# A transformer block on one core: another order of work on TensorE, VectorE, ScalarE and GpSimd in its attention part

## What is computed

```
x = L0_attn_x                                   # (8, 512, 256)
h = _layernorm(x) * (1 + ca) + sa
x = x + ga * _L0_attn_ref(h, w_qkv, w_out)      # q, k = elu(rope(q * SCALE)) + 1, elu(rope(k * SCALE)) + 1
   # for each row: kv += k v^T; ks += k; out = q kv / max(q ks, 1e-6)
h = _layernorm(x) * (1 + cb) + sb
x = x + gb * _L0_ffn_ref(h, router_w, w1, w2)   # top 2 of 8 experts
```

## Time and profile before

| | before |
|---|---|
| median of three runs | 779.57 us |
| lowest and highest | 779.16 and 779.76 us |
| span of the profiled execution | 776.0 us |
| PE, DVE, ACT, POOL busy over the span | 92%, 81%, 74%, 67% |
| attention part (start to the last chunk's offset, by the trace) | about 336 us |
| 24 steps of it, from `f` of chunk 2 to `f` of chunk 26 | 228.6 us |

### The profile page before, as it was taken

How to read it: one execution, slowest core, us unless ns; L and a number is a source line. 1 busy time by engine, 2 the same in 40 slices (tenths; PEclk the granted TensorE clock), 3 DMA queues, 4 the chain that set the end, 5 groups by cost and what they waited for, 6 DMA issues and landing times.

```text
span 776.0 us, 24871 instructions
## 1 busy us (share of the span) xinstructions
...
## 2 busy tenths in 40 slices
...
GB/s 226 113 67 133 110 135 120 131 120 139 124 140 116 151 64 67 120 48 8 96 77 69 71 73 74 76 70 79 70 75 69 77 69 76 76 72 76 72 21 1
DMA packets 52854, 69.27 MB, mean 89 GB/s; under 512 B 8864, under 2 KB 44080, under 8 KB 52736
## 3 DMA queue, kind: packets, MB, share of 16 engines
q0 software_dynamic: 18176, 27.06, 18.6%
...
## 4 chain that ended last, share of the span: by engine, by line
PE 51%; DVE 2%; POOL 2%; issue 1%; DMA 1%; ACT 0%; POOLq 0%; DVEq 0%; ACTq 0%
PE hidden L1457 16%; PE bank L1475 15%; PE hidden L1459 8%; PE bank L1477 8%; PE bank L1292 2%; POOL mod_b L960 1%; PE bank L1309 0%; DMA xt<-ffn_rows,gi 0%; DMA out_dram<-x,si 0%; DVE stage L651 0%; PE bank L1300 0%; PE bank L1389 0%; POOL out_dram L1008 0%; DVE feat L652 0%; POOL mod_b L962 0%
## 5 line engine op out<-in xcount | busy, mean ns | idle before, releaser
L1457 PE MATMUL hidden<-qstT,w1hi_k 128*128 128x256 f16 x1136 | 197.9, 274 | 0.7 <-DVE qstT L755 0.7
L1459 PE MATMUL hidden<-qstT,w1lo_k 128*128 128x128 f16 x1136 | 193.6, 220 | 0.0
L1475 PE MATMUL bank<-w,amhi 128*128 x568 | 188.4, 379 | 0.1
L1477 PE MATMUL bank<-w,amlo 128*128 x568 | 154.8, 273 | 0.0
L1008 POOL DMA_INDIRECT out_dram<-x,si x71 | 115.2, 1622 | 38.8 <-issue 25.8
L791 DVE TENSOR_TENSOR amlo<-am,amhi 128x512 f16<-128x512 f32 x142 | 98.3, 693 | 49.2 <-ACT am L1168 49.2
L1457 PEld LDWEIGHTS hidden<-qstT,w1hi_k 128*128 x1136 | 111.7, 98 | 14.0 <-issue 1.1
L1459 PEld LDWEIGHTS hidden<-qstT,w1lo_k 128*128 x1136 | 111.6, 98 | 0.2
L1309 PE MATMUL bank<-wq,hT 128*128 128x512 f32 (+1 forms) x256 | 98.8, 511 | 1.3 <-DVE hT L524 1.2
L1475 PEld LDWEIGHTS bank<-w,amhi 128*128 128x128 f16 x568 | 55.6, 98 | 59.9 <-issue 0.4
L1167 ACT ACTIVATE amhi<-am 128x512 f16<-128x512 f32 x142 | 88.1, 620 | 0.3 <-DVE am L785 0.3
...
...
## 6 DMA issues: line engine op xcount, KB each, us to landing
...
```

Source lines behind the costliest of these rows:

```text
L1457: t.matmul(dst.rearrange("p (q n) -> p q n", q=2), w1s[0][k][g][:, w_], both, start=(k == 0), stop=False)
L1459: last = t.matmul(dst[:, P:2 * P], w1s[1][k][g][:, w_], both[:, 0, :], start=False, stop=(k == KT - 1))
L1475: t.matmul(y[:, :], ghi[:, m.p, c_m], w2s[mt // 2][:, bass.ds(w_, 2 * D)], start=(mt == 0), stop=False)
L1477: last = t.matmul(y[:, D:2 * D], glo[:, m.p, c_m], w2s[mt // 2][:, bass.ds(w_, D)], start=False, stop=(mt == MT - 1))
```

## The change

Four tables of order are replaced (`ORDER_PE`, `ORDER_DVE`, `ORDER_POOL`, `ORDER_ACT`), and so are all five `CLOSING_` lists. The works themselves, their instructions, their number, `ORDER_SP` and the opening tables' contents stay. One wait is added, in `residual`: before `x1` of chunk m is written, `xn2` of chunk m - 2 must have read the buffer. The core of the diff:

```
-ORDER_PE = (("aT", 4), ("ear", 3), ("sc1", 3), ("pj", 4), ("hT", 0), ("h2T", 6), ("Tk", 2), ("pv0", 3), ("v", 0),
-            ("Tq", 2), ("pv1", 3), ("lg", 6), ("state", 2), ("sc0", 2), ("qk", 0))
+ORDER_PE = (("pj", 4), ("hT", 0), ("h2T", 6), ("Tk", 2), ("pv0", 3), ("v", 0), ("Tq", 2), ("lg", 6), ("pv1", 3),
+    ("state", 2), ("sc0", 2), ("qk", 0), ("aT", 3), ("ear", 2), ("sc1", 2))
...
-CLOSING_DVE = (("f", 26), ("st2", 23), ("sl0", 25), ("st", 28), ("mv", 28), ("stl", 25), ("mv2", 23), ("st", 29),
...
-    ("ve", 35), ("rec", 31), ("at", 31), ("nb", 35), ("wlo", 30), ("x1", 31), ("st2", 31), ("mv2", 31), ("ve", 36),
-    ("nb", 36), ("wlo", 31))
...
+    ("nb", 34), ("sl1", 31), ("mv2", 30), ("ve", 35), ("den", 31), ("rec", 31), ("at", 31), ("nb", 35), ("x1", 31),
+    ("st2", 31), ("mv2", 31), ("ve", 36), ("nb", 36))
...
             def residual(m):

                 wait(dve, a_["pj"], m.n + 1)
+                wait(dve, a_["xn2"], m.n - 1)
                 wait(dve, s_out[m.p], 16 * m.pairs)
                 v.tensor_tensor(x1[:, m.p, :], bank[2][:, D:2 * D], x_slot(m), ALU.add).then_inc(a_["x1"], 1)
```

More of the change, by code:

```diff
@@ L58 @@
 Q_SCALE = WS * float(HD ** -0.25)
-ORDER_PE = (("aT", 4), ("ear", 3), ("sc1", 3), ("pj", 4), ("hT", 0), ("h2T", 6), ("Tk", 2), ("pv0", 3), ("v", 0),
-            ("Tq", 2), ("pv1", 3), ("lg", 6), ("state", 2), ("sc0", 2), ("qk", 0))
-ORDER_DVE = (("st2", 5), ("st", 0), ("mv2", 5), ("mv", 0), ("ve", 0), ("f", 2), ("sl0", 3), ("nb", 0), ("rope", 1),
-             ("stl", 3), ("x1", 4), ("hTe", 0), ("sl1", 3), ("wlo", 1), ("vlo", 0), ("den", 3), ("rec", 3), ("at", 3))
-ORDER_POOL = (("rs", 0), ("shk", 2), ("slo", 2), ("wb", 4), ("R", 1), ("xm2", 5), ("h2", 5))
@@ L65 @@
-ORDER_ACT = (("exp", 2), ("sh0", 3), ("shq", 2), ("sth", 3), ("aTe", 4), ("xn", 0), ("sh1", 3), ("whi", 1),
-             ("kTs", 2), ("xn2", 5), ("vhi", 0), ("h2Te", 6), ("qTs", 2), ("lge", 6))
+ORDER_PE = (("pj", 4), ("hT", 0), ("h2T", 6), ("Tk", 2), ("pv0", 3), ("v", 0), ("Tq", 2), ("lg", 6), ("pv1", 3),
+    ("state", 2), ("sc0", 2), ("qk", 0), ("aT", 3), ("ear", 2), ("sc1", 2))
+ORDER_DVE = (("den", 4), ("st", 0), ("rec", 4), ("mv2", 5), ("at", 4), ("f", 2), ("mv", 0), ("ve", 0), ("sl0", 3),
+    ("nb", 0), ("stl", 3), ("rope", 1), ("x1", 4), ("hTe", 0), ("sl1", 3), ("wlo", 1), ("vlo", 0), ("st2", 4))
@@ L67 @@
+ORDER_POOL = (("xm2", 6), ("h2", 6), ("wb", 5), ("shk", 2), ("rs", 0), ("slo", 2), ("R", 1))
+ORDER_ACT = (("qTs", 3), ("lge", 7), ("exp", 2), ("sh0", 3), ("sth", 3), ("shq", 2), ("aTe", 4), ("xn", 0),
+    ("whi", 1), ("sh1", 3), ("xn2", 5), ("kTs", 2), ("h2Te", 6), ("vhi", 0))
 ORDER_SP = (("ldx", 0), ("modg", 6), ("modb", 7), ("so", 6), ("ro", 6), ("ld", 0), ("modgb", 6), ("gb", 6))
-OPENING_PE = {0: (("hT", 0), ("qk", 0), ("v", 0)), 1: (("hT", 0), ("mod1", 0), ("v", 0), ("qk", 0))}
+OPENING_PE = {0: (("hT", 0), ("qk", 0), ("v", 0)),
+    1: (("hT", 0), ("mod1", 0), ("v", 0), ("qk", 0))}
@@ L69 @@
 OPENING_DVE = {0: (("st", 0), ("mv", 0), ("ve", 0), ("nb", 0), ("hTe", 0)),
-               1: (("st", 0), ("mv", 0), ("ve", 0), ("nb", 0), ("rope", 1), ("vlo", 1), ("hTe", 0), ("wlo", 1), ("vlo", 0))}
-OPENING_ACT = {0: (("xn", 0),), 1: (("xn", 0), ("vhi", 1), ("whi", 1), ("vhi", 0))}
+    1: (("st", 0), ("mv", 0), ("ve", 0), ("nb", 0), ("rope", 1), ("vlo", 1), ("hTe", 0), ("wlo", 1), ("vlo", 0))}
+OPENING_ACT = {0: (("xn", 0),),
+    1: (("xn", 0), ("vhi", 1), ("whi", 1), ("vhi", 0))}
 CLOSING = 28
-CLOSING_PE = (("aT", 24), ("ear", 25), ("sc1", 25), ("pv0", 25), ("Tk", 26), ("state", 26), ("pj", 24), ("Tq", 26),
[11 rows of a table removed]
@@ L85 @@
-CLOSING_DVE = (("f", 26), ("st2", 23), ("sl0", 25), ("st", 28), ("mv", 28), ("stl", 25), ("mv2", 23), ("st", 29),
[13 rows of a table removed]
-CLOSING_POOL = (("shk", 26), ("slo", 26), ("rs", 28), ("R", 27), ("xm2", 23), ("h2", 23), ("rs", 29), ("shk", 27),
[5 rows of a table removed]
[L105 to L111, removed]
-    ("sh0", 29), ("sh1", 29), ("aTe", 28), ("vhi", 31), ("kTs", 30), ("exp", 31), ("qTs", 30), ("shq", 31),
[4 rows of a table removed]
@@ L117 @@
-CLOSING_SP = (("so", 22), ("ldx", 28), ("ldx", 29), ("so", 23), ("ro", 22), ("ldx", 30), ("ld", 28), ("ro", 23),
[4 rows of a table removed]
+CLOSING_PE = (("pv0", 25), ("h2T", 22), ("Tk", 26), ("pj", 24), ("hT", 28), ("Tq", 26), ("state", 26), ("lg", 22),
[10 rows of a table added]
+CLOSING_DVE = (("mv2", 23), ("den", 24), ("st", 28), ("mv", 28), ("rec", 24), ("ve", 28), ("f", 26), ("at", 24),
+    ("sl0", 25), ("nb", 28), ("rope", 27), ("stl", 25), ("st", 29), ("sl1", 25), ("wlo", 27), ("f", 27), ("hTe", 28),
+    ("den", 25), ("x1", 24), ("rec", 25), ("st2", 24), ("mv2", 24), ("mv", 29), ("ve", 29), ("at", 25), ("sl0", 26),
+    ("nb", 29), ("rope", 28), ("vlo", 28), ("stl", 26), ("sl1", 26), ("wlo", 28), ("f", 28), ("hTe", 29), ("x1", 25),
[4 rows of a table added]
+    ("mv2", 27), ("den", 28), ("wlo", 30), ("ve", 32), ("rec", 28), ("vlo", 31), ("at", 28), ("stl", 29), ("nb", 32),
[5 rows of a table added]
```

19 lines of the change are left out of this document (added), and 60 rows, old and new, of tables (CLOSING_ACT, CLOSING_DVE, CLOSING_PE, CLOSING_POOL).

## The result

The changed kernel takes **805.3 us** (median of four runs, 803.97 to 806.27) against 779.66 (779.16 to 779.93). The ratio is 1.0329, with a 95% interval from 1.0317 to 1.0341: 3.3% slower. The profiled execution has a span of 803.6 us against 776.0. The spans lie 27.6 apart and the medians 25.6, because the profiled execution of the kernel before was a quick one. What follows compares the two spans.

A forecast was written before the change was run, and what follows sets the result against it. Three engines within 5% of full; a round of waits through VectorE, GpSimd and TensorE sets the 9.45 us step. 24 x 1.35 = 32.4, less 1.3, is +31.1: median 779.6 to 811 us, range 794 to 822.

The forecast's parts named there:

- `ve` shut out by `shk`: VectorE: `ve` waits for GpSimd's cast `shk` to end and finishes 1.40 us after `f` starts, not 0.99.
- `nb` behind `slo`: VectorE: `nb`, due at 2.46, waits for the first half of GpSimd's `slo` and ends at 3.36 us.
- `rs` at 0.70: GpSimd: `rs` takes 0.70 us instead of 1.07, since only `sl0` (PSUM) runs beside it.
- ScalarE's round: ScalarE from `nb`: `xn` at 3.48, `kTs` at 6.48, next `f` due at 10.46 us; VectorE's 10.81 decides.
- `wlo` split: VectorE: `wlo` waits 0.15 us for `xm2`, then `h2` comes between its halves, costing 0.53.
- `vlo` to `f`: VectorE, end of step: this stretch shrinks from 2.41 to 1.71 us, between 1.6 and 1.9.
- Counted against 9.45: Steady steps: 10.8 us each, 1.35 more than an undisturbed 9.45, times 24 gives 32.4; single stalls left as they are.
- The ends: Closing lists: `wlo` of chunk 31 off the path gives back 1.3 us; the rest alike within 3 us.
- Span to median: Whole kernel: span from 776.0 to 807.1 us, median from 779.6 to 811 us.
- `lg` ahead of `pv1`: TensorE: puts `den` back by at most 0.6 us, to 8.4; free, as VectorE comes there at about 9.8.
- no collision: Rival: `ve`, `nb` and `wlo` all escape in the steady steps, -4.2 us, 775 us in all; chance 0.13.

The follow-up runs named there:

- run 2: Changed kernel with VectorE's `mv` and `ve` back ahead of `f` in the steady steps; 810.76 us (kernel before: 783.73).
- Run 4: Changed kernel, same orders, with `ve` and `nb` each written as two one-element instructions; 787.85 us (kernel before: 783.73).
- run 9: Kernel before with only GpSimd's `rs` moved behind `shk` in the steady steps; 811.19 us against 782.41.
- runs 3: Changed kernel with `xn2` moved to the end of ScalarE's steady step; 806.87 us (kernel before: 783.73).
- run 5: Changed kernel with one-element `ve` and `nb`, and `xn2` at the end of ScalarE's step; 789.51 us against 786.56 before, ratio 1.0033.
- run 1: Changed kernel with GpSimd's `rs` back ahead of `shk` in the steady steps; 793.57 us, kernel before 783.73, ratio 1.0125.
- runs 6: Changed kernel with one-element `ve` and `nb`, and `mv`, `ve`, `rs` and ScalarE's order back as before; 795.47 us against 786.56, ratio 1.0131.
- 11: Changed kernel with one-element `ve`, `nb`; `mv`/`ve` ahead of `f`, `rs` of `shk`, `pv1` of `lg`; ScalarE's order back; 781.71 us, ratio 0.9990.

## Why the prediction was right, and where its sizes were off

The forecast of 811 (794 to 822) holds 805.3, and the mechanism is the one forecast. Point by point:

- **`ve` shut out by `shk`: right.** Forecast end 1.40, measured 1.38, and `ve` took 0.57 where about 0.6 was expected. One row of a tenth of a us had told it. But run 2 shows that this part of the chain is worth nothing by itself.
- **`nb` behind `slo`: right.** Forecast end 3.36, measured 3.31. Run 4 shows that the two collisions cost 0.92 a step, and run 9 that moving `rs` is enough for the larger.
- **`rs` at 0.70: right.**
- **ScalarE's round: right in kind.** `xn` at 3.40 (3.48 forecast), `kTs` at 6.34 (6.48), `exp` done for an `f` at 10.36 (10.46). It does not decide, as forecast, but it lies only 0.2 below VectorE's bound, and runs 3 and 5 ran into it.
- **`wlo` split: right, mis-sized.** I added 0.15 of waiting ahead of its first half to the 0.53. From the work behind `nb` to `vlo` it took 5.67 where 5.14 + 0.68 = 5.82 was forecast. `h2` came between the halves, as forecast. `xm2` did start ahead of `wlo`, by 0.65, and ended 0.08 after `wlo`'s start, but the first half took its 0.68 all the same, so the 0.15 was not there. In run 1, where `xm2` started only 0.2 to 0.3 ahead, the first half did wait: it took 1.06.
- **`vlo` to `f`:** 1.68 measured, 1.71 forecast. So a step is 10.58 and not 10.81: 0.05 from `nb`, 0.15 from `wlo`, 0.03 here.
- **Counted against 9.45: a mistake.** The prediction says that the few long steps of the kernel before are left as they are. They are not. The step that was 1.07 longer than its neighbours has no like in the changed kernel, and of those that were 0.3 longer one is left, with 10.81; the later VectorE may cover them, which no run tested. The term should have been 10.81 less the mean of 9.53. That is 24 x 0.08 = 1.9 of the 7.5 us by which the steps were put too high (32.4 against 24.9); the shorter step has the rest.
- **The ends.** The 1.3 us of `wlo` came back as forecast. Not in the sum were +1.0 ahead of chunk 2, for which nothing was allowed, and +2.9 in the closing, just inside the 3 us allowed for it. That these 3.9 made up for half of the 7.5 is luck: had the kernel not had them, the forecast of the span would have been 7.5 us too high, and not 3.5.
- **Span to median: a mistake.** 3.6 us was added to the span as what lies around it. The changed kernel's profiled execution took 2.1 more than its span (805.69 and 803.6), and its median lies 1.7 above that span. The rest of the 3.6 was the quick profiled execution of the kernel before. This is 1.9 of the 5.7 us between 811 and 805.3.
- **`lg` ahead of `pv1`: free here,** but runs 6 and 11 show by what: `h2Te`. The reason given, that VectorE comes to `den` late anyway, was not the whole of it.

The rival "no collision" at 775 is wrong because `ve` and `nb` both collide; but run 4, in which neither does, gives 1.005 times the time of before and not 0.994. Its `wlo` was still split (1.81), which the rival had excluded, and run 5 without the split had the same average step. In neither did the new order give anything.

Left open: in which stretch the usual execution of the kernel before takes the 2 us that its profiled one did not.
